# GpSimd's indirect transfers in a four-layer mixture-of-experts kernel: a wait for the preceding pair's landing in place of a wait for the tile two slots back

## The chip, the cores and the metric

The kernel runs on one core of one Trainium2 chip. The metric is the device time of one execution in microseconds (us), as the median of three runs. The engines are named as in the profile: PE is TensorE (PEld its weight loads), DVE VectorE, ACT ScalarE, POOL GpSimd, SP SyncE. Here SP issues all plain DMAs, and POOL issues all indirect ones.

## The reference

Six sublayers are applied to x, which is 8 x 256 rows of 128 columns (2048 rows):

```python
x = x + 0.5 * _L0_ffn_ref(_layernorm(x), ...)
x = x + _L0_attn_ref(_layernorm(x), ...)
x = x + 0.5 * _L0_ffn_ref(_layernorm(x), ...)
x = x + 0.5 * _L1_ffn_ref(_layernorm(x), ...)
x = x + _L1_attn_ref(_layernorm(x), ...)
x = x + 0.5 * _L1_ffn_ref(_layernorm(x), ...)
```

Each of the four feed-forward sublayers is a mixture of 8 experts in which every row goes to its two best:

```python
xn = rms_norm(x, norm_scale)
scores = xn @ w_router.T
scores_topk, idx = jax.lax.top_k(scores, 2)
up = moe_linear(xf, ids, w_up)             # xf: each row twice, row i gets W[ids[i]]
u, gate = jnp.split(up, 2, axis=-1)
down = moe_linear(u * jax.nn.silu(gate), ids, w_down)
out = jnp.sum(down * weights, axis=-2)
return out + skip
```

The hidden width is 256 in the first two and 352 in the last two. L0 attention is squared-ReLU attention within 256 rows, L1 attention is a causal linear attention with 16 heads.

## The kernel before

The 2048 rows are four groups of 512 (group index b or g). A feed-forward sublayer s (0 to 3) of one group is a **phase**: the group's 1024 (row, expert) pairs are sorted by expert into 15 tiles of 128 rows, a tile per **slot**. There are 16 phases in the order sublayer by sublayer and group by group within one, so 240 slots (SLOTS). While PE multiplies the tiles of one phase, all other work (routing, attention, combining) of the other groups is placed between the slots by tables of offsets, ROUTE, ATTENTION and COMBINE, counted in slots from the end of a group's last phase. Each engine has one instruction stream written in the order of the slots, and executes it in order; semaphores tie the streams together.

The path of one group from one phase to the next touches POOL several times:

- **Gather** (`gather`, L514, slots 3 to 6 after the phase's end): y_rows<-y_dram. The expert results, stored in DRAM by SP, are fetched back in row order, by eight indirect transfers of 128 rows of 512 bytes: four pairs, each pair of one block c of 128 rows (first and second expert). Semaphore gathered[b][c // 2]. In the last phase part of the tiles is gathered by `gather_early` (L531), which had no wait for a slot.
- **Combine** on DVE (L722), in two halves h0 and h1, each of which waits for two pairs of the gather. For sublayer 0 the halves are 8 and 10 slots after the phase's end.
- **Attention**, after sublayers 0 and 2. POOL computes a_rstd (L538) with a power function, and for L1 attention four products of 128x512 (L547, attention<-attention), from which ACT makes kv_hi and DVE kv_lo, which PE sums.
- **Route** for the next sublayer: POOL computes b_rstd (L486), then come the normalised rows rms_out (DVE L708), scores, top two, and the row positions pos (DVE L832, rows_of; semaphore pos_ready).
- **Scatter** (L495, route's offset "scatter"): rows_dram<-rms_out. The 512 normalised rows are written into sorted order in DRAM, by four pairs of indirect transfers. Semaphore scattered[g]. SP then waits for all eight and loads the rows back (L386, rows<-rows_dram), four tiles at a time, in the same queue that issues the loads of the expert weights (L400, up<-in_up, four slots ahead).

POOL's stream holds 16 scatters and 15 gathers of four pairs and the four pairs of gather_early, 128 pairs in all. Below, scatter k and gather k are those of phase k, counted from 0.

Before every pair stands `pace(t)`: the pair of slot t waits until ACT's SiLU (L581, semaphore silu_done) has finished the tile of slot t-2. It holds nothing else back: where POOL is late, the pairs follow one another at once.

## Time and profile before

| | us |
|---|---|
| median of 3 runs | 762.65 |
| the three runs | 762.65, 761.97, 771.69 |
| span of the profiled execution, first to last instruction | 751.7 |
| median less that span (start and end of an execution, outside the span) | 10.95 |
| PE busy in the span | 616.4 |
| POOL busy in the span | 318.2 |

The time of the profiled execution as a whole is not listed beside its span, so the difference to the median stands for what lies around it. POOL is busy while it generates the descriptors of a transfer; the time in which the DMA engines move the data and signal the semaphore is in no engine's busy time.

### The profile page before, as it was taken

How to read it: one execution, taken by the hardware profiler on the slowest of the kernel's cores; microseconds unless marked ns; L12 is line 12 of the kernel's file. 1: busy time of each engine (PE TensorE's matmuls, PEld its weight loads, DVE VectorE, ACT ScalarE, POOL GpSimd, SP SyncE). 2: the span in 40 equal slices, each digit the busy share in tenths (PEclk: the TensorE clock that was granted, in tenths of full speed). 3: DMA queues.
4: the chain of work that ended last, by engine and by line, in shares of the span. 5: the costliest groups of instructions: out<-in, count | busy, mean ns of one | idle time of the engine just before them, and what ended most of it. 6: DMA issues, size and time to landing. Idle time of an engine off the chain costs nothing.

```text
span 751.7 us, 15429 instructions
## 1 busy us (share of the span) xinstructions
PE 616.4 (82%) x4590; PEld 567.3 (75%) x4590; DVE 404.3 (54%) x1385; ACT 263.8 (35%) x549; POOL 318.2 (42%) x352
## 2 busy tenths in 40 slices
PE   2597888959969598767879779798898989888987
PEld 1386777848759488667779779697887979877987
DVE  6744343815528146342445335297796876954446
ACT  2233342523524333322333223443634435323331
POOL 4535444261441633544350534514615736344134
PEclk9999899989989989786988889899999999998999
DMA  7578576635626347564765657475564575556853
GB/s 253 149 221 260 170 204 212 194 110 148 187 75 199 116 143 222 155 208 135 216 197 149 190 156 214 136 207 164 173 201 132 159 232 156 181 166 224 261 157 76
DMA packets 113268, 133.57 MB, mean 178 GB/s; under 512 B 10931, under 2 KB 76227, under 8 KB 112806
## 3 DMA queue, kind: packets, MB, share of 16 engines
q1 hardware_dynamic: 104998, 115.79, 52.6%
q0 software_dynamic: 8192, 16.79, 7.4%
q8 instruction: 42, 0.69, 0.4%
q14 instruction: 36, 0.29, 0.1%
HBM read 103.83 MB, written 28.71 MB: 176 GB/s over the span
## 4 chain that ended last, share of the span: by engine, by line
PE 59%; DVE 12%; another core or an unknown queue 12%; issue 7%; ACT 7%; POOL 2%; DMA 0%; DVEq 0%; ACTq 0%
PE up_gate L1029 18%; PE up_gate L1022 11%; PE y L983 10%; PE side L1110 3%; PE y L985 3%; PE side L1044 2%; ACT hidden L581 2%; POOL b_rstd L486 2%; PE side L1060 2%; DVE hidden L686 2%; PE side L1126 2%; ACT x_res L598 2%; DVE rms_out L708 1%; DVE kv_lo L872 1%
## 5 line engine op out<-in xcount | busy, mean ns | idle before, releaser
L686 DVE TENSOR_TENSOR hidden<-up_gate,hidden 128x256 f32<-128x256 f32 (+1 forms) x240 | 115.7, 488 | 252.0 <-ACT hidden L581 125.0
L1029 PE MATMUL up_gate<-rows_T,up 128*128 128x128 f32 x1440 | 194.5, 286 | 26.0 <-issue 14.0
L1029 PEld LDWEIGHTS up_gate<-rows_T,up 128*128 128x128 f32 x1440 | 181.4, 200 | 32.4 <-issue 19.6
L495 POOL DMA_INDIRECT rows_dram<-rms_out,rows_of x128 | 130.1, 1016 | 171.8 <-DVE rows_of L832 90.5
L581 ACT ACTIVATE hidden<-up_gate 128x256 f32<-128x256 f32 (+1 forms) x240 | 104.3, 436 | 279.8 <-PE up_gate L1022 103.0
L514 POOL DMA_INDIRECT y_rows<-y_dram,rows_of x120 | 121.9, 1016 | 85.3 <-ACT hidden L581 46.1
L1022 PE MATMUL up_gate<-rows_T,up 128*128 128x128 f32 x960 | 139.7, 291 | 16.5 <-ACT rows_T L586 9.6
L1022 PEld LDWEIGHTS up_gate<-rows_T,up 128*128 128x128 f32 x960 | 126.7, 203 | 24.7 <-issue 22.1
L983 PE MATMUL y<-down,hidden 128*128 x480 | 78.7, 288 | 8.2 <-DVE hidden L686 6.0
L486 POOL TENSOR_TENSOR b_rstd<-b_var,minus_half 128x8 f32<-128x8 f32 x16 | 26.8, 1674 | 121.6 <-DVE b_var L703 121.5
L983 PE MATMUL y<-down_a,hidden 128*128 x480 | 76.3, 283 | 0.0
L983 PEld LDWEIGHTS y<-down,hidden 128*128 128x128 f32 x480 | 67.3, 202 | 11.1 <-issue 11.1
L586 ACT ACTIVATE rows_T<-side,norm 128x512 f32<-128x512 f32 x64 | 42.2, 660 | 75.8 <-remote 39.8
L983 PEld LDWEIGHTS y<-down_a,hidden 128*128 128x128 f32 x480 | 66.4, 200 | 0.0
L574 ACT ACTIVATE y_tile<-y 128x512 f32<-128x512 f32 x64 | 36.4, 569 | 35.8 <-PE y L985 22.0
L985 PE MATMUL y<-down_b,hidden 96*128 x240 | 47.9, 281 | 0.0
L1044 PE MATMUL side<-ident,rows 128*128 128x128 f32 x236 | 38.3, 284 | 2.5 <-DVE scores L770 1.5
L985 PEld LDWEIGHTS y<-down_b,hidden 96*128 96x128 f32 x240 | 37.9, 198 | 0.0
L1110 PE MATMUL side<-attention 128*128 128x256 f32 x64 | 20.8, 492 | 19.4 <-DVE attention L888 18.4
L1055 PE MATMUL side<-ident,rms_out 128*128 128x128 f32 x64 | 12.4, 326 | 29.6 <-DVE rms_out L708 15.3
L1110 PEld LDWEIGHTS side<-attention 128*128 128x128 f32 x64 | 15.9, 256 | 23.4 <-DVE attention L888 18.9
L1055 PEld LDWEIGHTS side<-ident,rms_out 128*128 128x128 f32 x64 | 8.4, 165 | 31.4 <-issue 23.3
(188 smaller groups left out, 700.4 us busy)
## 6 DMA issues: line engine op xcount, KB each, us to landing
up<-in_up SPq DMA_DIRECT2D x120, 352.0 KB
up<-in_up SPq DMA_DIRECT2D x120, 256.0 KB
rows<-rows_dram SPq DMA_DIRECT2D x47, 256.0 KB, 3.0
y_dram<-y_tile SPq DMA_DIRECT2D x45, 256.0 KB, 2.5
rows_dram<-zeros SPq DMA_DIRECT2D x12, 256.0 KB, 3.6
rows<-rows_dram SPq DMA_DIRECT2D x16, 192.0 KB
y_dram<-y_tile SPq DMA_DIRECT2D x15, 192.0 KB
rows_dram<-rms_out,rows_of POOLq DMA_INDIRECT x128
```

The lines of the kernel that those rows point to most:

```text
L486: pool.tensor_tensor(b_rs[:, :], b_ve[:, :], mhalf[:, :], ALU.pow).then_inc(b_rstd, 1)
L495: pool.indirect_dma_start(out=xg_d[g], out_offset=bass.IndirectOffsetOnAxis(ap=pos[g][:, at:at + 1], axis=0), in_=xs(Z, GROUPS[g][c // TB] ...
L514: pool.indirect_dma_start(out=gath[b % 2][:, (TB * k2 + c) * P:(TB * k2 + c + 1) * P], out_offset=None, in_=y_d[g], in_offset=bass.Indirec ...
L581: act.activation(hid[n % 4][:, 0:w], src, ACT.Silu).then_inc(silu_done, 1)
L586: act.activation(xgT[r % 3][:, 0:n * P], S[2][:, 0:n * P], ACT.Copy, scale=wn[:, LAYER[s]:LAYER[s] + 1]).then_inc(s2_free, 1)
L686: dve.tensor_tensor(h, u, h, ALU.mult).then_inc(mult_done, 1)
L983: last = pe.matmul(y, hid[n % 4][:, c * P:(c + 1) * P], w, start=(c == 0), stop=(l == 0 and c == 1))
L985: last = pe.matmul(y, hid[n % 4][0:96, 2 * P:3 * P], dn1b[:, bass.ds(v * P, P)], start=False, stop=True)
L1022: last = pe.matmul(U[q % 3][:, i * P:(i + 1) * P], upW[n % RING][:, at:at + P], rows_, start=True, stop=True)
L1029: last = pe.matmul(U[q % 3][:, c * P:(c + 1) * P], upW[n % RING][:, at + c * P:at + (c + 1) * P], rows_, start=True, stop=True)
L1044: last = pe.transpose(S[2][:, c * P:(c + 1) * P], xg[r % 4][:, c * P:(c + 1) * P], ident[:, :])
L1110: last = pe.matmul(S[1 - q][:, c * SEQ:(c + 1) * SEQ], R[4 + q][:, t * HID + c * P:t * HID + (c + 1) * P], R[6 + q][:, t * SEQ:(t + 1) * S ...
```

## The change

`pace` and its wait on silu_done go. In its place every pair remembers its semaphore and the count that the semaphore has when both its transfers have landed (`pair_landed`), and before the next pair POOL waits for that (`wait_for_pair`). gather_early, which had no pacing, gets the same wait. The other waits (pos_ready, y_stored, combined) stay.

```diff
-            def pace(t):
-
-                if 1 < t <= SLOTS:
-                    pool.wait_ge(silu_done, t - 1)
+            landing = []
+
+            def pair_landed(sem, count):
+
+                landing[:] = [(sem, count)]
+
+            def wait_for_pair():
+
+                for sem, count in landing:
+                    pool.wait_ge(sem, count)
...
-                    pace(t)
+                    wait_for_pair()
                     for at in (2 * c, 2 * c + 1):
                         pool.indirect_dma_start(out=xg_d[g], out_offset=bass.IndirectOffsetOnAxis(ap=pos[g][:, at:at + 1], axis=0),
                                                 in_=xs(Z, GROUPS[g][c // TB], c % TB * P, P), in_offset=None,
                                                 bounds_check=TILES[g] * P - 1, oob_is_err=False).then_inc(scattered[g], 16)
+                    pair_landed(scattered[g], 32 * (CH[g] * (turns(s1, g) - 1) + c + 1))
...
-                    pace(t)
+                    wait_for_pair()
                     i = TB * GROUPS[g].index(b) + c
                     for k2 in range(2):
...
+                    pair_landed(gathered[b][c // 2], 16 * TB * s + 32 * (c % 2 + 1))
...
+                wait_for_pair()
                 for k2 in range(2):
                     at = 2 * c + k2
...
+                pair_landed(gathered[b][c // 2], 16 * TB * s + 32 * (c % 2 + 1))
```

No instruction changes its place on any engine; only what POOL's pairs wait for differs. Two places of POOL's stream show it. The first is the round of POOL in the L0 attention part, from the last pair of scatter 5 (rows_dram1) over gather 3 (y_rows1<-y_dram3) to the first pair of scatter 6. Before:

```order
L495 DMA rows_dram1<-rms_out,rows_of1 1920x128 [waits silu_done]
L495 DMA rows_dram1<-rms_out,rows_of1 1920x128
L514 DMA y_rows1<-y_dram3,rows_of3 128x128 [waits y_stored3,combined,y_stored2,silu_done,y_stored1,y_stored0]
L514 DMA y_rows1<-y_dram3,rows_of3 128x128
L514 DMA y_rows1<-y_dram3,rows_of3 128x128 [waits silu_done]
...
L486 TENSOR_TENSOR b_rstd<-b_var,minus_half 128x8 [waits b_var]
L538 TENSOR_TENSOR a_rstd<-a_var,minus_half 128x4 [waits ln1_var]
L495 DMA rows_dram2<-rms_out,rows_of2 1920x128 [waits silu_done,pos_ready]
```

And after:

```order
L501 DMA rows_dram1<-rms_out,rows_of1 1920x128 [waits scattered1]
L501 DMA rows_dram1<-rms_out,rows_of1 1920x128
L521 DMA y_rows1<-y_dram3,rows_of3 128x128 [waits y_stored3,combined,y_stored2,scattered1,y_stored1,y_stored0]
L521 DMA y_rows1<-y_dram3,rows_of3 128x128
L521 DMA y_rows1<-y_dram3,rows_of3 128x128 [waits gathered3_0]
...
L492 TENSOR_TENSOR b_rstd<-b_var,minus_half 128x8 [waits b_var]
L548 TENSOR_TENSOR a_rstd<-a_var,minus_half 128x4 [waits ln1_var]
L501 DMA rows_dram2<-rms_out,rows_of2 1920x128 [waits gathered3_1,pos_ready]
```

Each silu_done has become a wait for the landing of the pair before, also across the border from scatter to gather; b_rstd and a_rstd stand behind all eight pairs as before.

The second place is in the L1 attention part, the end of gather 10 (y_rows0<-y_dram2), scatter 12 (rows_dram0) and the first two products of L1 attention. Before:

```order
L514 DMA y_rows0<-y_dram2,rows_of2 128x128 [waits silu_done]
L514 DMA y_rows0<-y_dram2,rows_of2 128x128
L495 DMA rows_dram0<-rms_out,rows_of0 1920x128 [waits silu_done,pos_ready]
L495 DMA rows_dram0<-rms_out,rows_of0 1920x128
L547 TENSOR_TENSOR attention<-attention 128x512 [waits v_ready,phi_ready]
```

And after:

```order
L521 DMA y_rows0<-y_dram2,rows_of2 128x128 [waits gathered2_1]
L521 DMA y_rows0<-y_dram2,rows_of2 128x128
L501 DMA rows_dram0<-rms_out,rows_of0 1920x128 [waits gathered2_1,pos_ready]
L501 DMA rows_dram0<-rms_out,rows_of0 1920x128
L557 TENSOR_TENSOR attention<-attention 128x512 [waits v_ready,phi_ready]
```

The products are queued behind the gather and the scatter's first pair in both; the pairs ahead of them now wait for landings.

## Rows read from the trace of the kernel before

**Rows 1.** The page: span, busy time, chain by engine, hardware DMA queue.

```profile
span 751.7 us, 15429 instructions
PE 616.4 (82%) x4590; PEld 567.3 (75%) x4590; DVE 404.3 (54%) x1385; ACT 263.8 (35%) x549; POOL 318.2 (42%) x352
PE 59%; DVE 12%; another core or an unknown queue 12%; issue 7%; ACT 7%; POOL 2%; DMA 0%; DVEq 0%; ACTq 0%
q1 hardware_dynamic: 104998, 115.79, 52.6%
```

**Rows 2.** The chain that ended last: start us, us, what.

```profile
200.81 3.20 another core or an unknown queue
...
207.48 6.49 another core or an unknown queue
```

**Rows 3.** Timeline of POOL, one round: start us, us, engine line op.

```profile
196.90 1.06 POOL L495 DMA_INDIRECT rows_dram<-rms_out,rows_of  x1 [6.86 <-DVE rows_of L832]
198.27 0.99 POOL L495 DMA_INDIRECT rows_dram<-rms_out,rows_of  x1 [0.30 <-issue]
...
207.23 1.04 POOL L514 DMA_INDIRECT y_rows<-y_dram,rows_of  x1 [0.30 <-issue]
...
219.37 1.00 POOL L514 DMA_INDIRECT y_rows<-y_dram,rows_of  x1 [0.31 <-issue]
229.14 1.67 POOL L486 TENSOR_TENSOR b_rstd<-b_var,minus_half 128x8 f32<-128x8 f32 x1 [8.78 <-DVE b_var L703]
...
245.09 1.06 POOL L495 DMA_INDIRECT rows_dram<-rms_out,rows_of  x1 [6.86 <-DVE rows_of L832]
```

**Rows 4.** Timeline of DVE: the positions for which scatter 6 waited.

```profile
244.11 0.17 DVE L832 CAST rows_of<-rows_of_f 128x8 int32<-128x8 f32 x1
```

**Rows 5.** Timelines: last transfer of a set, and who waited for its landing.

```profile
548.17 0.99 POOL L495 DMA_INDIRECT rows_dram<-rms_out,rows_of  x1 [0.30 <-issue]
550.44 0.38 SPq L386 DMA_DIRECT2D rows<-rows_dram  x1
...
689.55 0.98 POOL L495 DMA_INDIRECT rows_dram<-rms_out,rows_of  x1 [0.31 <-issue]
694.60 0.38 SPq L386 DMA_DIRECT2D rows<-rows_dram  x1
...
742.83 0.99 POOL L531 DMA_INDIRECT y_rows<-y_early,early_rows_of  x1 [0.30 <-issue]
745.72 0.61 DVE L722 SCALAR_TENSOR_TENSOR x_res<-y_rows,w_first,x_res 128x128 f32<-128x128 f32 x2 [2.16 <-DMA y_rows<-y_early,early_rows_of]
```

**Rows 6.** Timelines: first scatter, combine h1 of gather 0, scatter 3.

```profile
19.62 1.21 POOL L495 DMA_INDIRECT rows_dram<-rms_out,rows_of  x1 [7.96 <-issue]
...
95.41 0.59 DVE L722 SCALAR_TENSOR_TENSOR x_res<-y_rows,w_first,x_res 128x128 f32<-128x128 f32 x2
...
100.11 1.06 POOL L495 DMA_INDIRECT rows_dram<-rms_out,rows_of  x1 [0.27 <-issue]
```

**Rows 7.** Timeline of POOL: first pairs of scatters 7 and 11.

```profile
292.15 1.07 POOL L495 DMA_INDIRECT rows_dram<-rms_out,rows_of  x1 [13.33 <-ACT hidden L581]
...
459.98 1.02 POOL L495 DMA_INDIRECT rows_dram<-rms_out,rows_of  x1 [19.28 <-DVE rows_of L832]
```

**Rows 8.** Timeline of POOL, L1 attention part, scatters 12 and 15.

```profile
486.48 2.10 POOL L547 TENSOR_TENSOR attention<-attention 128x512 f32<-128x512 f32 x2
...
519.48 1.09 POOL L514 DMA_INDIRECT y_rows<-y_dram,rows_of  x1 [0.44 <-issue]
...
534.16 1.02 POOL L495 DMA_INDIRECT rows_dram<-rms_out,rows_of  x1 [1.74 <-ACT hidden L581]
...
545.35 1.08 POOL L547 TENSOR_TENSOR attention<-attention 128x512 f32<-128x512 f32 x1
...
567.85 1.08 POOL L514 DMA_INDIRECT y_rows<-y_dram,rows_of  x1 [0.45 <-issue]
...
678.28 1.02 POOL L495 DMA_INDIRECT rows_dram<-rms_out,rows_of  x1 [0.31 <-issue]
```

**Rows 9.** Timelines: first pair of gather_early; the last addition.

```profile
732.15 1.00 POOL L531 DMA_INDIRECT y_rows<-y_early,early_rows_of  x1 [11.43 <-issue]
...
748.28 0.69 DVE L733 TENSOR_TENSOR x_res<-x_res,side 128x512 f32<-128x512 f32 x1 [1.30 <-PE side L1173]
```

## The prediction

> **What bounds the kernel now.** I read the page first. PE is busy 82% of the span and stands for 59% of the chain that ended last; POOL is busy 42% and stands for 2% [rows 1]. Read so, POOL's transfers are far from the bound. But 12% of the chain is "another core or an unknown queue" [rows 1], some 90 us that no engine's work explains, so I looked where in the chain it lies. It comes in pieces such as the 3.20 us at 200.81 and the 6.49 us at 207.48 [rows 2]. In both, ACT had finished and PE's tile had been issued, and the tile's signal came late. The timeline of POOL shows what goes on beside: both lie in a dense run of indirect transfers, one every 1.3 us, that begins at 196.90 and goes over from scatter 5 to gather 3 [rows 3]. The other long pieces that I looked up lie in such runs too. So the kernel before pays up to 90 us for something that goes with many indirect transfers in flight, and the change, which never has more than two in flight, may give that back. This speaks for the change and is in the sum below, in full.
>
> Against it stands a time that no busy row shows: how long a pair takes until its landing is known to POOL. It decides the sum.
>
> **The price of a pair.** Generating two transfers takes from 196.90 to 198.27 + 0.99 = 199.26 [rows 3]: 2.35 us. The landing, from the end of the second generation to whoever waited for it: 550.44 - 549.16 = 1.28 us, 694.60 - 690.53 = 4.07 us, and for a gather 745.72 - 743.82 = 1.90 us [rows 5]. The low end is a quiet moment of the queues, the high end one with loads beside. The hardware queue is at work for 52.6% of the span [rows 1], so neither end is typical; I take the gather row, 1.9 us. Restart: pos was written at 244.11 + 0.17 = 244.28 and scatter 6, which waited for it, began at 245.09 [rows 3, 4]: 0.8 us, which a dense run hides in its gap of 0.3. Together P = 2.35 + 1.9 + 0.8 = 5.05, taken as 5.0 us from pair to pair, where a dense run needs 2 x 1.3 = 2.6. Bounds for P as a mean: 2.35 + 1.28 + 0.8 = 4.4 below, and with half of the pairs at each of the two scatter rows 2.35 + 2.7 + 0.8 = 5.8 above.
>
> This is where a page bears on it. "DMA: Bandwidth & Descriptors" of the Trainium skill, section "Anatomy of one DMA — SWDGE (gpsimd) path", gives such a transfer a fixed 2.0 us, most of it the write's receipt, plus bytes over 436e3. For the 64 KB here that is 2.15 us from issue, an estimate from that page, against 550.44 - 548.17 = 2.27 in the quiet row and 5.05 in the loaded one [rows 5]: the trace agrees with it only in the quiet case. By the page P would be 1.3 + 2.15 + 0.8 = 4.25 (estimate), and the total would come out near 741 us.
>
> **What hangs on POOL's queue.** 128 pairs at 5.0 us are 640 us, where POOL was busy 318 us, generation of all of them included [rows 1]. So POOL turns from an engine with 58% idle into one in which nearly every round is a chain. I follow the queue in six parts. PE stalls are assumed gone everywhere.
>
> (a) *Start to scatter 3.* Scatters 0 to 2 and gather 0 follow each other without a gap: the positions for scatters 1 and 2 are ready by the time POOL gets there, and the waits on silu_done that had held scatter 2 are gone. From 19.62 there are 15 steps of P, the last pair's generation and landing (2.35 + 1.9), then combine h1, after which scatter 3 came 100.11 - 95.41 = 4.70 later, over a_rstd [rows 6]. 19.6 + 75 + 4.25 + 4.7 = 103.6 against 100.1: **+3.5**.
>
> (b) *Scatter 3 to scatter 7, four rounds, 192.0 us* (100.11 to 292.15) [rows 6, 7]. In each, b_rstd stands behind all eight pairs, and the next positions depend on it: from b_rstd to the next scatter 245.09 - 229.14 = 15.95 us [rows 3], in which PE runs at its pace without a stall, so it stays. Before, POOL had ended its pairs at 220.37 and b_rstd waited 8.8 us for its data [rows 3]; that slack is eaten. A round is 7 x 5.0 + 2.35 + 15.95 = 53.3 us; four are 213.2: **+21.2**. The stalls lie inside the eight pairs, so that their end buys nothing here.
>
> (c) *Scatter 7 to scatter 11, four rounds, 167.8 us* (292.15 to 459.98) [rows 7]. No attention; b_rstd stands between scatter and gather, and the chain from it to the next positions, without its stalls, runs beside the gather and is no longer than that. A round is then 8 pairs, 40.0 us: 160 in all, **-7.8**. This is what of the stalls is earned.
>
> (d) *Scatter 11 to scatter 12, 74.2 us* (459.98 to 534.16). The products of L1 attention wait behind scatter 11 and gather 9: they come 37.35 us after the scatter's start, where it was 486.48 - 459.98 = 26.5. From there to gather 10 PE's pace rules, 519.48 - 486.48 = 33.0, and the gather's four pairs take 20 us where scatter 12 came 14.7 after it [rows 7, 8]: 37.35 + 33.0 + 20 = 90.35, **+16.2**.
>
> (e) *Scatter 12 to scatter 15, three rounds, 144.1 us* (534.16 to 678.28). The last product comes behind the third pair, 2 x 5.0 + 2.35 = 12.35 after the start, against 545.35 - 534.16 = 11.19; the product itself and two of its fellows lie in the landing waits. From it to the next gather 567.85 - 545.35 = 22.5, unchanged, then 20 us of gather [rows 8]. Three times 54.85 is 164.6: **+20.4**.
>
> (f) *End.* The rows of the last phase are loaded 3 x 5.0 + 2.35 + 1.9 = 19.25 us after scatter 15 starts, against 694.60 - 678.28 = 16.3 [rows 5, 8]; SP already waited for them, with the weight loads queued behind: **+2.9**. gather_early takes 19.25 against 745.72 - 732.15 = 13.6; of these 5.7 us about 1.2 are hidden, since the last addition waited 1.30 for PE [rows 5, 9]: **+4.5**.
>
> Sum: 3.5 + 21.2 - 7.8 + 16.2 + 20.4 + 2.9 + 4.5 = +60.9. Span 751.7 + 60.9 = 812.6, and with the 10.95 us around it **823.6 us, 824**. What is removed, a wait that POOL's sequencer makes, costs nothing itself.
>
> Of the chain that I sum, 15 + 28 + 32 + 11 + 18 + 6 = 110 steps are P. Each 0.1 us of P is 11 us, and with P at 5.0 - 61/110 = 4.45 the change does nothing.
>
> **Rivals.**
>
> 1. *The landings are quick.* With the pairs spread out and PE often idle, the weight loads leave the queues quiet, and P is near its lower bound 4.4: +60.9 - 66 = -5, 757 us, no change. For it: the quiet row recurs wherever SP had stopped issuing. Against: the same weights must still be moved, and the scatters start while PE runs and asks for them. The page's 4.25, and its total of 741, would be this rival's extreme.
>
> 2. *The stalls are what counts, and POOL isn't the chain.* The other side: the 12% go, 90 us [rows 1], and landings stay hidden under the schedule's slack. 762.65 - 90 = 673; it needs eight pairs and the work behind them within a round that is 48.2 us now (196.90 to 245.09) and would be some 38 without the two pieces of rows 2: 7P + 18.3 below 38 asks for P below 2.9, less than the generation and the quiet landing. A gain of over 2% asks for 15.3/110 below the even point, P under 4.3, which is under the lower bound, unless my chains are wrong: if in (b) b_rstd could go ahead of the gather's last pairs, for instance, which its place in the queue forbids. It is the case in which I have misread what depends on what.
>
> 3. *The stalls stay.* If PE's late signals come with every indirect transfer and not with the number in flight, (b) is unchanged, but (c) doesn't shrink: its stalls of some 10 us a round come beside waits already there. With half of that on the path +20, 844 us.
>
> 4. *The change does nothing* because the pairs' landing is as a rule past when the next is due. 745.72 and 550.44 speak against it: a dense run issues every 1.3 us, far ahead of any landing.
>
> **How the numbers follow.** My forecast (P from 4.6 to 5.4, 780 to 868): 0.60. Rival 3: 0.12. Rival 1 and 4 together: 0.15. Rival 2, in full or in part: 0.13. Within 2% (747.4 to 777.9), about what a measurement of this kernel can tell from no change, lie rivals 1 and 4: 0.15; faster is rival 2: 0.13; slower the rest, 0.72. The range reaches down to rival 1 and up over rival 3 to P of 5.4: 755 to 868.
>
> **What the profile after would show.** POOL's transfers in pairs, 4.4 to 5.8 us from pair to pair, each with an idle time before it put down to DMA or to issue of 2 to 3 us, in place of 0.3. The share "another core or an unknown queue" under 4%, with more of the chain on POOL and DMA. In (b), b_rstd right behind the last gather transfer, with DVE idle before L708 and L722, and rounds of 53 us. In (d), L547 some 37 us after scatter 11's start. I am wrong if the mean step is under 4.45, if b_rstd still waits for b_var in (b), or if unexplained pieces of the chain stay.

## The result, and the profile after

| | before | after |
|---|---|---|
| median, us | 762.31 (759.75 to 771.69, 4 runs) | 878.22 (871.85 to 883.42, 4 runs) |
| ratio | | 1.149, 95% interval 1.141 to 1.158 |
| profiled execution, its time, us | not on record | 871.85 |
| its span, us | 751.7 | 870.1 |

The change makes the kernel 15% slower, by 116 us; 61 had been forecast. In the experiments below a median is of all runs, while a ratio and its interval leave out runs more than 1.5% above the quickest of their kernel. The page of the changed kernel, to be held against [rows 1]: span, busy time, hardware queue, chain by engine, and three groups (busy and mean ns, then idle time before them and what ended most of it).

```profile
span 870.1 us, 15430 instructions
PE 622.5 (72%) x4590; PEld 578.2 (66%) x4590; DVE 405.3 (47%) x1385; ACT 268.5 (31%) x549; POOL 317.7 (37%) x352
q1 hardware_dynamic: 104998, 115.79, 45.0%
DMA 44%; POOL 18%; issue 18%; PE 14%; DVE 4%; POOLq 1%; ACT 1%; DVEq 0%; ACTq 0%
L501 POOL DMA_INDIRECT rows_dram<-rms_out,rows_of x128 | 130.1, 1017 | 239.9 <-DMA rows_dram<-rms_out,rows_of 134.0
L521 POOL DMA_INDIRECT y_rows<-y_dram,rows_of x120 | 121.9, 1016 | 197.4 <-DMA y_rows<-y_dram,rows_of 135.4
L718 DVE TENSOR_SCALAR rms_out<-x_res,b_meanvar,b_rstd 128x128 f32<-128x128 f32 x64 | 17.9, 347 | 132.9 <-POOL b_rstd L492 132.9
```

POOL is busy for the same 318 us, and yet the chain has changed hands: PE went from 59% to 14%, and DMA (that is, POOL waiting for landings) from 0 to 44%. "Another core or an unknown queue", 12% before, isn't in the list any more. These are waits in ACT and DVE that the view of waits puts down to "remote"; the piece of 6.49 us in [rows 2] is one. In the kernel before it looked so:

```profile
203.35 1.05 PE L1022 MATMUL up_gate<-rows_T,up 128*128 128x128 f32 x8
213.99 0.38 ACT L581 ACTIVATE hidden<-up_gate 128x256 f32<-128x256 f32 x1 [6.51 <-remote]
```

This SiLU (L581) waits for one semaphore only, the one that PE raises behind the eight products; PE's records of them end at 204.40, and ACT went on at 213.99. Below these waits are called unexplained.

In the changed kernel the idle time ended by landings, 134.0 + 135.4, is 269 us. Busy shares show none of this; the idle columns do.

One round of (b) on POOL, the counterpart of [rows 3]:

```profile
202.37 1.00 POOL L521 DMA_INDIRECT y_rows<-y_dram,rows_of  x1 [2.86 <-DMA y_rows<-y_dram,rows_of]
...
207.89 1.00 POOL L521 DMA_INDIRECT y_rows<-y_dram,rows_of  x1 [3.22 <-DMA y_rows<-y_dram,rows_of]
...
212.53 1.00 POOL L521 DMA_INDIRECT y_rows<-y_dram,rows_of  x1 [2.34 <-DMA y_rows<-y_dram,rows_of]
213.83 1.00 POOL L521 DMA_INDIRECT y_rows<-y_dram,rows_of  x1 [0.30 <-issue]
214.86 1.68 POOL L492 TENSOR_TENSOR b_rstd<-b_var,minus_half 128x8 f32<-128x8 f32 x1
...
232.49 1.06 POOL L501 DMA_INDIRECT rows_dram<-rms_out,rows_of  x1 [8.53 <-DVE rows_of L842]
```

Pairs start 5.52 and 4.64 us apart. b_rstd has lost its wait of 8.78 [rows 3] and stands right behind the gather's last transfer. The same round on DVE:

```profile
198.83 0.16 DVE L713 SCALAR_TENSOR_TENSOR b_var<-b_var,b_meanvar 128x4 f32<-128x4 f32 x1
...
216.57 1.12 DVE L718 TENSOR_SCALAR rms_out<-x_res,b_meanvar,b_rstd 128x128 f32<-128x128 f32 x4 [16.47 <-POOL b_rstd L492]
```

b_var was there at 198.99, and DVE stood idle for 16.47 us until POOL came round to b_rstd.

The steps' length varies with what the DMA engines carry. The third and the fourth pair of scatter 0, then rows of a round of (c), from scatter 8 to scatter 9:

```profile
30.11 0.97 POOL L501 DMA_INDIRECT rows_dram<-rms_out,rows_of  x1 [2.03 <-DMA rows_dram<-rms_out,rows_of]
...
34.39 0.97 POOL L501 DMA_INDIRECT rows_dram<-rms_out,rows_of  x1 [2.03 <-DMA rows_dram<-rms_out,rows_of]
...
386.55 1.08 POOL L501 DMA_INDIRECT rows_dram<-rms_out,rows_of  x1 [2.90 <-DMA y_rows<-y_dram,rows_of]
...
393.56 0.97 POOL L501 DMA_INDIRECT rows_dram<-rms_out,rows_of  x1 [3.95 <-DMA rows_dram<-rms_out,rows_of]
...
399.20 0.97 POOL L501 DMA_INDIRECT rows_dram<-rms_out,rows_of  x1 [3.39 <-DMA rows_dram<-rms_out,rows_of]
...
429.40 1.02 POOL L501 DMA_INDIRECT rows_dram<-rms_out,rows_of  x1 [3.99 <-DMA y_rows<-y_dram,rows_of]
```

30.11 to 34.39 is a quiet step, 4.28 us; 386.55 to 393.56 is 7.01, 393.56 to 399.20 is 5.64, and the round's eight pairs take 42.85 in all, 5.36 each. The same stretches in the view by windows (us, then busy us and instructions of PE, PEld, DVE, ACT and POOL, granted clock, busy share of the DMA engines, GB/s):

```profile
30.11:34.39 4.28, 2.34 (x22) 2.06 (x21) 0.83 (x4) 1.38 (x4) 1.94 (x3) 1.00 0.09 31
386.55:393.56 7.01, 5.13 (x44) 4.76 (x43) 3.51 (x17) 2.68 (x6) 2.09 (x3) 1.00 0.63 208
```

The DMA engines are busy for 0.09 of the quiet step and for 0.63 of the long one. It is so throughout: of the 99 steps from a scatter pair to a scatter pair or a gather pair to a gather pair, the 11 below 4.5 us have a mean share of 0.19, the 28 of 6 us and more one of 0.75. By the formula that "DMA: Bandwidth & Descriptors" of the Trainium skill, section "Anatomy of one DMA — SWDGE (gpsimd) path", gives for one transfer, a step is 4.25 us (estimate): the trace agrees with this in the quiet row, 4.28, and in none of the loaded rows shown.

The borders of the six parts of the forecast, the first pairs of scatters 3, 7 and 11, the first product behind scatter 11, and scatters 12 and 15:

```profile
115.72 1.11 POOL L501 DMA_INDIRECT rows_dram<-rms_out,rows_of  x1 [0.21 <-issue]
341.84 1.06 POOL L501 DMA_INDIRECT rows_dram<-rms_out,rows_of  x1 [14.57 <-DVE rows_of L842]
523.24 1.02 POOL L501 DMA_INDIRECT rows_dram<-rms_out,rows_of  x1 [4.20 <-DVE rows_of L842]
565.00 1.08 POOL L557 TENSOR_TENSOR attention<-attention 128x512 f32<-128x512 f32 x1
618.68 1.02 POOL L501 DMA_INDIRECT rows_dram<-rms_out,rows_of  x1 [4.06 <-DMA y_rows<-y_dram,rows_of]
788.93 1.07 POOL L501 DMA_INDIRECT rows_dram<-rms_out,rows_of  x1 [6.03 <-DMA y_rows<-y_dram,rows_of]
```

| part | before | after | change | forecast |
|---|---|---|---|---|
| (a) to scatter 3 | 100.1 | 115.7 | +15.6 | +3.5 |
| (b) 3 to 7 | 192.0 | 226.1 | +34.1 | +21.2 |
| (c) 7 to 11 | 167.8 | 181.4 | +13.6 | -7.8 |
| (d) 11 to 12 | 74.2 | 95.4 | +21.3 | +16.2 |
| (e) 12 to 15 | 144.1 | 170.3 | +26.1 | +20.4 |
| (f) to the end | 73.4 | 81.2 | +7.7 | +7.4 |
| span | 751.7 | 870.1 | +118.4 | +60.9 |

### The profile page after: what moved, and what is told of

Its sections match the earlier page's. It is cut to its first block, busy times and chain, and to the rows that moved or that the text cites. A ratio compares the mean times of both kernels' runs of the same rounds, so it can differ in the third digit from the quotient of the medians.

```text
span 870.1 us, 15430 instructions
## 1 busy us (share of the span) xinstructions
PE 622.5 (72%) x4590; PEld 578.2 (66%) x4590; DVE 405.3 (47%) x1385; ACT 268.5 (31%) x549; POOL 317.7 (37%) x352
## 4 chain that ended last, share of the span: by engine, by line
DMA 44%; POOL 18%; issue 18%; PE 14%; DVE 4%; POOLq 1%; ACT 1%; DVEq 0%; ACTq 0%
DMA y_rows<-y_dram,rows_of 20%; DMA rows_dram<-rms_out,rows_of 20%; POOL rows_dram L501 7%; POOL y_rows L521 7%; PE up_gate L1039 5%; PE y L993 3%; POOL b_rstd L492 2%; PE up_gate L1032 2%; DMA y_rows<-y_early,early_rows_of 1%; DMA y_dram<-y_tile 1%; POOL attention L557 1%; PE y L995 1%; PE side L1054 1%; DMA rows<-rows_dram 1%; DVE rms_out L718 1%
## 5 line engine op out<-in xcount | busy, mean ns | idle before, releaser
L501 POOL DMA_INDIRECT rows_dram<-rms_out,rows_of x128 | 130.1, 1017 | 239.9 <-DMA rows_dram<-rms_out,rows_of 134.0
L1039 PE MATMUL up_gate<-rows_T,up 128*128 128x128 f32 x1440 | 197.7, 290 | 11.5 <-DVE hidden L696 7.5
L1039 PEld LDWEIGHTS up_gate<-rows_T,up 128*128 128x128 f32 x1440 | 185.4, 204 | 17.8 <-DVE hidden L696 8.8
L521 POOL DMA_INDIRECT y_rows<-y_dram,rows_of x120 | 121.9, 1016 | 197.4 <-DMA y_rows<-y_dram,rows_of 135.4
L1032 PE MATMUL up_gate<-rows_T,up 128*128 128x128 f32 x960 | 143.1, 297 | 5.0 <-issue 3.6
L1032 PEld LDWEIGHTS up_gate<-rows_T,up 128*128 128x128 f32 x960 | 130.9, 209 | 13.1 <-issue 10.8
L993 PEld LDWEIGHTS y<-down,hidden 128*128 128x128 f32 x480 | 69.6, 209 | 72.0 <-issue 72.0
L718 DVE TENSOR_SCALAR rms_out<-x_res,b_meanvar,b_rstd 128x128 f32<-128x128 f32 x64 | 17.9, 347 | 132.9 <-POOL b_rstd L492 132.9
L1065 PE MATMUL side<-ident,rms_out 128*128 128x128 f32 x64 | 15.3, 384 | 65.3 <-DVE rms_out L718 63.2
L1065 PEld LDWEIGHTS side<-ident,rms_out 128*128 128x128 f32 x64 | 10.6, 196 | 67.4 <-DVE rms_out L718 56.7
L603 ACT ACTIVATE z_T<-side,norm 128x512 f32<-128x512 f32 x16 | 11.0, 686 | 135.7 <-PE side L1065 129.4
L492 POOL TENSOR_TENSOR b_rstd<-b_var,minus_half 128x8 f32<-128x8 f32 x16 | 26.9, 1681 | 71.0 <-DVE b_var L713 70.9
L1054 PEld LDWEIGHTS side<-ident,rows 128*128 128x128 f32 x236 | 28.6, 146 | 36.2 <-DMA rows<-rows_dram 21.2
## 6 DMA issues: line engine op xcount, KB each, us to landing
rows<-rows_dram SPq DMA_DIRECT2D x16, 192.0 KB
y_dram<-y_tile SPq DMA_DIRECT2D x15, 192.0 KB
```

Source lines behind the costliest of these rows:

```text
L492: pool.tensor_tensor(b_rs[:, :], b_ve[:, :], mhalf[:, :], ALU.pow).then_inc(b_rstd, 1)
L501: pool.indirect_dma_start(out=xg_d[g], out_offset=bass.IndirectOffsetOnAxis(ap=pos[g][:, at:at + 1], axis=0), in_=xs(Z, GROUPS[g][c // TB] ...
L521: pool.indirect_dma_start(out=gath[b % 2][:, (TB * k2 + c) * P:(TB * k2 + c + 1) * P], out_offset=None, in_=y_d[g], in_offset=bass.Indirec ...
L993: last = pe.matmul(y, hid[n % 4][:, c * P:(c + 1) * P], w, start=(c == 0), stop=(l == 0 and c == 1))
L1032: last = pe.matmul(U[q % 3][:, i * P:(i + 1) * P], upW[n % RING][:, at:at + P], rows_, start=True, stop=True)
L1039: last = pe.matmul(U[q % 3][:, c * P:(c + 1) * P], upW[n % RING][:, at + c * P:at + (c + 1) * P], rows_, start=True, stop=True)
```

## The experiments

Each set of kernels ran beside the kernel before on the same chip. In four of the five sets that took 756 to 762 us, in the second 644.5. This difference became the most telling measurement, and is taken up below. The sets in which the kernel before took 756 to 762 us are called the usual condition, the second set the quick one. The ratios are always to the kernel before of the same set.

**Set 1** (before: 757.2 us).

*nowait*: neither the old wait nor the new one.

```diff
-                if 1 < t <= SLOTS:
-                    pool.wait_ge(silu_done, t - 1)
+                return
```

> The kernel before without pace, and with no wait for a landing: the change's one half alone. Theory A (the 15% are the landing waits, in POOL's in-order queue): taking pace away costs little, 755 to 790 us, with the unexplained pieces of the chain (PE's late signals) as long as before or longer, since runs of transfers get denser. Theory B (the loss comes from pace having kept the transfers away from other work, and the landing wait only adds to it): 800 us or more.

782.2 us, ratio 1.031 (1.024 to 1.037), in theory A's range. Dropping the pacing alone costs 25 us, and the unexplained share of the chain rises to 16%: a queue that runs freely is worse than one that is paced. The changed kernel has no unexplained share, so these 3% aren't shown to be a part of its 15%.

*lag2*: a pair waits for the pair before the preceding one, four transfers in flight (the counts split over two semaphores).

```diff
-                landing[:] = [(sem, count)]
+                landing.append((sem, count))
...
-                for sem, count in landing:
-                    pool.wait_ge(sem, count)
+                if len(landing) > 1:
+                    pool.wait_ge(*landing[-2])
```

> The changed kernel, but each pair waits for the pair before the preceding one, so up to four transfers are in flight (the semaphores of scatters and gathers are split by pair parity). Theory A: a landing of 2 to 5 us lies beside the next pair's generation, the step from pair to pair falls from some 5.5 us to 2.6 to 3.5, and the total to 690 to 745 us if four in flight are too few for PE's late signals, 750 to 775 if they are enough for them. Theory B (pace's removal costs): 820 us or more.

754.8 us is the median of ten runs between 737 and 763, no clear difference from the kernel before (757.2); the ratio of 0.981 (0.974 to 0.988) rests on the two quickest of the ten. Pairs are 3.2 us apart in scatters and 2.8 in gathers in the mean, the chain of landings is gone, but 9% of the chain is still unexplained. One pair more in flight is worth over 120 us against the change.

*scatter_only*: the landing waits in the scatters only; the gathers have pace(t) again, gather_early none. The scatter's first pair no longer waits for the gather before it, nor the gather's for the scatter, so a wait at the border is in neither half.

> Landing waits between the pairs of a scatter only; the gathers keep pace, gather_early has no wait. Theory A: some six in ten of the added time, since the scatters are half of the pairs and their landings stand before gathers and products too, 805 to 835 us; PE's late signals come back only in the gathers. Rival: if the gathers' landings alone hold b_rstd and the combines, under 785 us.

769.8 us, 1.018 (1.013 to 1.023), the rival's number. That scatters cost little doesn't follow yet: 8% of the chain is unexplained here too, so the two effects are mixed.

*after_small*: the changed kernel with the loads of the up weights cut to 32 columns after the first six tiles of each layer (it leaves out most of these weights).

```diff
+                u = w if n < RING or LAYER1 <= n < LAYER1 + RING else PAD
-                sp.dma_start(upW[n % RING][:, 0:w], (up0, up1)[l][:, bass.ds(v * w, w)])
+                sp.dma_start(upW[n % RING][:, 0:u], (up0, up1)[l][:, bass.ds(v * w, u)])
```

> The changed kernel with the weight loads cut: after the first six tiles of either layer only 32 of 512 or 704 columns are loaded (the expert results are those of stale weights). Theory A' (the pair step was priced too low because the landing competes with the weight loads): every pair step falls to the quiet 4.3 us of scatters and 4.6 of gathers, and the total by some 110 x 1 us to 750 to 790 us. Rival (the landing is slow by itself, by its receipt from DRAM or POOL's restart): steps stay at 5.4 to 5.6 us on average and the total above 850 us.

816.7 us in one run, between the two. The hardware queue's share falls from 45.0% to 21.7%, and the 32 steps of (c) from 181.4 to 161.5 us, from 5.67 to 5.05 a step, where a quiet one is 4.28. The weight loads make about half of what a step takes beyond the quiet row; what the rest is was not told apart (the loads and stores of rows and results are still there). Neither A', which had the quiet step and 750 to 790 us, nor its rival came true.

**Set 2** (before: 644.5 us, 642.7 to 652.0, 11 runs).

*gather_only*: the counterpart of scatter_only.

```diff
                         if turns(s1, g) == 1:
                             pool.wait_ge(zero_stored[g], 16 * ((TILES[g] + 3) // 4))
-                    wait_for_pair()
+                    pace(t)
```

> The counterpart of scatter_only: only the pairs of the gathers and of gather_early wait for the pair before them, the scatters are paced as before. Theory S (slack): in each round one half of the cost is taken up by time that POOL had to spare (8.8 us before b_rstd in (b)), and only what goes beyond it counts. Gather steps of about 5.4 us: 3 us a round in (b), nothing in (c), 7 us before scatter 12 and in each of the three rounds of (e), 5 at the end: about +45, 785 to 820 us, so that this kernel and scatter_only together come to much less than the change. Rival S' (sum): a pair costs the same wherever it stands, and since scatter_only came out 13 us above the kernel before and the change 115, this kernel takes the rest, 845 to 870 us.

745.4 us, 1.156 (1.148 to 1.163). The numbers were written for a kernel before of 757; as a difference, +101 us, it is what rival S' had (88 to 113), and not what slack had (28 to 63). Set 4 takes this up again.

*one_flight*: every single transfer waits for the one before (shown for the scatters; the gathers got the like).

```diff
                     for at in (2 * c, 2 * c + 1):
+                        if at % 2:
+                            pool.wait_ge(scattered[g], 32 * (CH[g] * (turns(s1, g) - 1) + c) + 16)
```

> The changed kernel with every single transfer waiting for the one before, so twice as many landings. Theory A (the cost is the number of landing steps on POOL's chain, at some 2.8 us each beyond a generation with its gap): some 110 to 118 steps more, each about 2.8 us, 1150 to 1220 us. Rival B (the landings take long because of what is in flight beside them, and get as quick as the quiet ones, 1.3 to 1.9 us, when everything thins out): 1.5 us or less a step more, 1000 to 1080 us.

1138.4 us in one run, 12 us short of theory A's range and far from B's: 262 us over the changed kernel's 876 (measured in set 4) for 110 more landings on the chain, 2.4 us each. The pair steps of a set grew from 5.5 and 5.4 us to 7.5 and 7.8. Its granted clock is lower too, 0.784 where the changed kernel has 0.866, so not all of the 2.4 need be landing.

*hoist*: b_rstd before the third pair of the gather.

```diff
-                if o == route_at(s1, b)["root"]:
+                if o == route_at(s1, b)["root"] - (3 if s1 == 1 else 0):
```

> The changed kernel with b_rstd of the four rounds of (b) put between the second and the third pair of the gather, in place of behind the fourth. Its data is ready by then (b_var stands at 198.99 us in the round in which b_rstd starts at 214.86). Theory H, as in the prediction: b_rstd is what heads the way to the next positions, so it and all that follows come 10 to 11 us earlier in each of four rounds: 825 to 840 us. Rival H' (the combine): the same DVE stream has both halves of the combine, which wait for the gather's last pair, between rms_out and the positions, so only the 2 to 3 us between the last landing and the end of the combine are saved: 860 to 870 us.

856.7 us, 1.326 (1.318 to 1.334), 3 us under H' and far from H. One round of it on DVE:

```profile
207.18 1.11 DVE L718 TENSOR_SCALAR rms_out<-x_res,b_meanvar,b_rstd 128x128 f32<-128x128 f32 x4 [9.59 <-POOL b_rstd L492]
...
218.23 0.61 DVE L732 SCALAR_TENSOR_TENSOR x_res<-y_rows,w_first,x_res 128x128 f32<-128x128 f32 x2 [7.98 <-DMA y_rows<-y_dram,rows_of]
```

Counted from the round's first scatter (175.45 here, 177.52 in the changed kernel), rms_out comes 7.3 us earlier than at 216.57, and the second half of the combine, behind it in DVE's stream, waits 7.98 us for the gather's last landing. This round is as long as before, 55.0 us in both. b_rstd was held up, but it was not alone in that.

*lag2_pace*: lag2 with pace(t) kept beside it.

> lag2 (a pair waits for the pair before the preceding one) with the old wait for the tile two slots back kept beside it. Theory C (what lag2 gained, it gained by fewer transfers in flight, and what it lost, nothing): the pacing spreads the runs further and the late signals of PE get rarer still: 735 to 750 us, faster than lag2. Rival D (the pacing adds waits to a queue that is late already): 752 to 765 us, no better than lag2's 754.84.

661.4 us, 1.025 (1.019 to 1.031). Both theories had been written for a kernel before of 757, and neither number came; beside 644.5 even this limit costs. The chain of gather_only here, and under it that of the kernel before as it ran in set 3 (before_again):

```profile
PE 29%; DMA 22%; POOL 17%; issue 16%; DVE 10%; ACT 4%; POOLq 1%; SPq 0%; DVEq 0%; ACTq 0%
```

```profile
PE 59%; DVE 14%; another core or an unknown queue 9%; issue 9%; ACT 7%; POOL 2%; DMA 0%; DVEq 0%; ACTq 0%
```

None of the four kernels traced in set 2 has a wait for "remote", and none of their chains an unexplained share (that of lag2_pace covers only the last 8% of its span).

**Set 3** (before: 762.3 us) repeated the main kernels; the quick condition didn't come back.

> The kernel before once more, for a trace of it on the chip on which it took 644.5 us, where all runs until then had shown 752 to 772. Theory X (the late signals of PE inside the dense runs of transfers, 12% of the chain in the first trace, are the whole difference, and that chip doesn't show them): a span of about 643 us and a share of another core or an unknown queue under 1%. Rival Y (the chips differ in the clock alone): the share stays near 12%, and PE's busy time differs in the ratio of the clocks. On a chip of the first kind both expect 750 to 765 us and 12%.

759.6 us, with an unexplained share of 9% where 12% had been expected: a condition of the usual kind, on which both theories say the same.

> The changed kernel beside the kernel before on this chip. Theory X: the changed kernel hangs on POOL's chain of landings, which the late signals hardly touch, so that its time is the same on either kind of chip, 860 to 880 us; where the kernel before takes 644.5 the ratio is then 1.33 to 1.37, where it takes 757 it is 1.14 to 1.16. Rival Y: both kernels get faster by the same ratio of 0.85, and the changed one takes about 740 us on the quicker chip.

879.8 us, 1.147 (1.139 to 1.156).

> lag2 beside the kernel before on this chip. Theory X: what lag2 gained (0.981) it gained on the late signals, so where they are absent only its cost is left, as in lag2_pace: 1.01 to 1.04 of the kernel before. Rival: lag2 is better in itself, 0.98 there too.

759.3 us, the median of ten runs between 740 and 765; 0.979 (0.970 to 0.988) is again the ratio of its two quickest.

> scatter_only beside the kernel before on this chip. Theory X: it came out at 1.018 only because it paid 4.4 of its own and won back a part of the late signals; where there are none its price shows in full: 1.05 to 1.12, and with the 1.156 of gather_only the two make up most of the change (1.33 and more). Rival S (slack, each half alone fits into idle time of POOL): 1.01 to 1.03.

781.3 us, 1.019 (1.011 to 1.027). Rival S had this; X's 1.05 to 1.12 was for the quick condition. In the usual condition the results of set 1 stand.

**Set 4** (before: 755.7 us) repeated those of set 2, to see them in the usual condition.

> gather_only beside the kernel before on this chip. Where the kernel before shows late signals of PE (757 to 762 us so far on three chips): theory X (the halves keep a part of the chain of landings and lose a part of the late signals) expects 785 to 815 us, 1.03 to 1.07, and with the 1.019 of scatter_only less than half of the change's 1.149, so that the cost comes mostly from both standing in one chain. Rival S' (sum): 845 to 870 us. Where the kernel before takes 644: 1.156 again.

755.1 us, 0.996 (0.992 to 1.001), lower than either theory had it: the same edit that costs 16% in set 2 costs nothing here.

> hoist beside the kernel before on this chip: b_rstd two gather pairs earlier in (b). Theory H' (the combine is what the next positions wait for, behind the gather's last landing): 2 to 4 us a round, 860 to 870 us against the 878 and 880 of the changed kernel, 1.13 to 1.14. Theory H (b_rstd alone): 825 to 840 us.

854.8 us, 1.132 (1.126 to 1.137), 5 us under H'; in set 2 it was 856.7.

> lag2 with the old pacing kept beside it, on this chip. Where the kernel before shows late signals: theory C (fewer in flight and the pairs spread) 730 to 750 us, 0.96 to 0.98; rival D (the pacing adds nothing but waits) 755 to 775. Where the kernel before takes 644: 1.025 again.

732.6 us, 0.972 (0.965 to 0.978), as theory C had it, and the best of all kernels in this condition.

> The changed kernel once more. On a chip with late signals 870 to 885 us. On one where the kernel before takes 644, theory X expects the chain of landings to be as long as ever, 860 to 880 us, 1.33 to 1.37; rival Y (everything is faster there) about 740.

876.3 us, 1.160 (1.151 to 1.168). hoist is 21.5 us quicker beside it. Its (b) takes 216 us, where the changed kernel's takes 235 here and 226 in the first trace, so 2 to 5 us a round in the mean; H' had 2 to 4. The rounds differ: in set 2, against the first trace, they gained 2.5, 0.0, 0.6 and 9.3 us. Why the last one gains what H had for all was not looked into.

**Set 5** (before: 757.8 us).

*slide*: as many in flight as in the change, two at most, but each single transfer waits for the last but one (counts over two semaphores).

```diff
-                    wait_for_pair()
                     for at in (2 * c, 2 * c + 1):
+                        wait_for_last_but_one()
...
```

> The changed kernel with its wait made sliding: each single transfer waits for the landing of the last but one, so that as many are in flight as in the changed kernel, two at most, but one is being generated while the other lands. Theory X (the cost is the length of a step, the gain the small number in flight): a pair takes 2 x (1.0 + about 1.9 + 0.8 restart) / 2 = 3.7 to 4.2 us in place of 5.4, so 110 steps save 130 to 190 us of the changed kernel's 876, and the late signals stay away as there: 700 to 745 us, below the kernel before where that takes 757. Where the kernel before takes 644: 690 to 720, slower than it. Rival Z (a wait for one landing costs what a wait for two does, since the landings are slow because of what else is in the queues): steps of 5 and more, 840 to 870 us.

768.7 us, 1.011 (1.005 to 1.017): 24 us over its range, 108 under the changed kernel of set 4. A piece of POOL's timeline and the chain:

```profile
357.43 1.02 POOL L522 DMA_INDIRECT y_rows<-y_dram,rows_of  x1 [0.31 <-issue]
359.43 1.01 POOL L522 DMA_INDIRECT y_rows<-y_dram,rows_of  x1 [0.99 <-DMA y_rows<-y_dram,rows_of]
360.75 1.01 POOL L522 DMA_INDIRECT y_rows<-y_dram,rows_of  x1 [0.30 <-issue]
362.73 1.01 POOL L522 DMA_INDIRECT y_rows<-y_dram,rows_of  x1 [0.97 <-issue]
```

```profile
DMA 40%; PE 21%; issue 17%; POOL 10%; DVE 10%; ACT 2%; POOLq 1%; DVEq 0%; ACTq 0%; SPq 0%
```

Here two transfers take 359.43 to 362.73 = 3.3 us; over the 32 steps of (c), 148.9 us, it is 4.65 a pair, where 3.7 to 4.2 had been expected. Rival Z, with 5 and more and 840 to 870 us, is refuted. No unexplained share, as in the changed kernel.

*slide_hoist*: both edits.

> slide with b_rstd two gather pairs earlier, as in hoist. Theory H': worth at most 2 to 4 us a round of (b) where POOL's chain still binds, 5 to 15 us below slide. Rival (with shorter steps b_rstd waits for its data there as in the kernel before, and holds up the last two gather pairs): equal to slide or up to 15 us slower.

752.3 us, 0.991 (0.987 to 0.996), 16 us under slide, just past the 5 to 15 of H', and just below the kernel before. It comes in (b), 204.9 us in slide and 183.8 here: 5.3 a round, over the 2 to 4 of H'.

**What the sets say together.** The view of waits of the kernel before, the unexplained ones in ACT and DVE (us in total, times, longest), and of lag2:

```profile
ACT hidden L581 <- remote: 60.6, 15, 7.2
ACT rows_T L586 <- remote: 39.8, 11, 6.0
DVE hidden L686 <- remote: 26.1, 7, 6.6
```

```profile
ACT hidden L592 <- remote: 46.4, 11, 7.7
ACT rows_T L597 <- remote: 32.0, 9, 6.0
DVE hidden L697 <- remote: 24.7, 5, 8.6
```

And of gather_only in set 4:

```profile
ACT hidden L595 <- remote: 40.5, 11, 6.7
ACT rows_T L600 <- remote: 26.9, 6, 7.4
```

Where they lie in time tells more. With the landing waits in the scatters only, all 23 unexplained waits of scatter_only stand beside a run of gathers; with them in the gathers only, all 18 of gather_only in set 4 stand beside a run of scatters. In the kernel before they stand beside both. One from scatter_only, and the gather transfer at its start:

```profile
267.57 1.00 POOL L526 DMA_INDIRECT y_rows<-y_dram,rows_of  x1 [0.31 <-issue]
277.95 0.94 ACT L593 ACTIVATE hidden<-up_gate 128x256 f32<-128x256 f32 x3 [10.82 <-remote]
```

| kernel | in flight | usual condition, us (unexplained waits) | set 2, us (unexplained waits) |
|---|---|---|---|
| nowait | any | 782 (yes) | |
| before | any, paced | 756 to 762 (yes) | 644.5 (no trace) |
| lag2 | 4 | 755 (yes) | |
| lag2_pace | 4, paced | 733 (yes) | 661 (none) |
| scatter_only | 2 in scatters | 770 (yes) | |
| gather_only | 2 in gathers | 755 (yes) | 745 (none) |
| slide | 2 | 769 (none) | |
| hoist | 2 | 855 (none) | 857 (none) |
| after | 2 | 876 to 880 (none) | |
| after_small | 2 | 817 (none) | |
| one_flight | 1 | | 1138 (none) |

In the usual condition five kernels with at most two transfers in flight (after, after_small, hoist, slide, slide_hoist) leave no such wait in seven traces, and every kernel with more in flight anywhere shows them. one_flight shows none either, but it ran in set 2, where no kernel does, whatever it has in flight. And only kernels with more than two in flight somewhere differ between the conditions: lag2_pace by 71 us, the kernel before by 113, gather_only by 10, hoist by 2.

My reading is that the change does two things of opposite sign. It takes away a loss that the kernel before has in the usual condition, 757 - 644.5 = 113 us. And it puts a chain of landings in its place, which costs, against a kernel without the loss, some 876 - 644.5 = 232 us. The net is the 116 to 121 measured. Two parts of this are argued and not shown. That the changed kernel takes 876 in the quick condition too rests on hoist, which took the same in both; it wasn't run there. And that the 113 are the unexplained waits isn't shown, since the kernel before has no trace in set 2. lag2_pace has one in both: its span is 67.9 us shorter in the quick condition, the granted clock 0.979 in place of 0.941, and 26.9 of the 67.9 are PE's own busy time (585.7 and 612.6 us for the same products). So a part of such a loss is time at a lower clock, and whether the waits bring the clock down or something else brings both was not tested. A low clock alone doesn't bring the waits: gather_only has 0.932 in set 2 and none of them.

The gather's half bears the reading out: it costs 101 us in set 2 and nothing in the usual condition, where it may pay for itself with the part of the loss that it ends. The rest would then be 131 us, for the scatters' half and the waits at the borders between the two; of that only the 13 to 19 of scatter_only in the usual condition were measured, and how much appears only when all form one chain isn't told apart.

That the unexplained waits come with more than two transfers in flight is shown for the usual condition; by what way a transfer holds them up, and what makes the condition, is open. Two of the sets carry the same chip number, one at 644.5 and one at 755.7, so the number alone doesn't tell them apart, and nothing in the traces names a cause.

## Why the prediction was wrong

The direction held, and so did the mechanism (POOL becomes a chain of landings, the unexplained pieces go); 878 lies above the range's end of 868.

**The step that failed is the price of a pair**, P = 5.0 us. In the sum it stands for 110 steps. Measured, these 110 take 600.4 us, 5.46 each: 50 of the 57.5 us by which the span was missed. In (c), where b_rstd and the positions hold up next to nothing, it is 181.4 / 32 = 5.67. I had taken the landing of the one gather row of [rows 5], 1.90 us, as the middle. The quiet scatter row was right (idle 2.03 = 1.28 + 0.8, to within 0.05), and typical rows are far from it: 2.9, 3.4, 3.95, where 1.9 + 0.8 = 2.7 had been assumed. With P at 5.45 the sum is 60.9 + 50 = 111 and the span 862.6; with the 6.3 of (b) below it is 868.9, where 870.1 was measured. The bound above, 5.8, held; the range of my forecast ended at P = 5.4, inside that bound, and so cut off the case that came.

Part by part: **(a)** +12 over the forecast, nearly all of it steps: scatter 3 came 12.1 us later than forecast, and the 15 steps took 86.3 us in place of 75. **(b)** +12.9 over it. The order of things was as told, b_rstd right behind the gather, DVE idle before rms_out. Half of the miss is steps; the other half is a second step of the prediction that failed, the way from b_rstd to the next scatter, which I had said "stays" at 15.95: in the round shown it is 232.49 - 214.86 = 17.63, and from 16.3 to 18.8 in the four, +6.3 in all. This stretch in the view by windows, before and after:

```profile
229.14:245.09 15.95, 15.40 (x129) 14.13 (x128) 13.69 (x62) 8.16 (x18) 2.68 (x2) 1.00 0.68 200
214.86:232.49 17.63, 13.03 (x92) 12.07 (x93) 13.32 (x60) 5.70 (x12) 2.68 (x3) 0.76 0.30 82
```

In the 10 us ahead of b_rstd PE was busy for 8.8 to 10 in all four rounds before; in the changed kernel it is busy for none of them in any round, and the granted clock falls to between 0.64 and 0.50 there. In the stretch behind b_rstd the clock, 1.00 in all four rounds before, is 0.74 to 0.79. Of the four, the longest (18.82 us) has the lowest clock, 0.74, and the shortest (16.25) the highest, 0.79. So the clock goes with the 6.3; that it makes them was not tested by a run. That b_rstd is the head was half of the truth: with it moved, the combine waits in its place (hoist), and a round gains 2 to 5 us in the mean, not 9. **(c)** is where the price of P turned the sign: forecast 40.0 a round against 41.95 before, measured 45.4. The gain I had booked there, -7.8, was the stalls' end; they did end, and the price of P took more than they gave. **(d)** The product came 565.00 - 523.24 = 41.8 after scatter 11, forecast 37.35; the 4.4 are the miss but for 0.7. **(e)** +5.7 over 18 steps, 0.3 a step. **(f)** right to 0.3, in part by luck: the three steps of its scatter took 13.7 us in place of 15, the three of gather_early 15.9.

**A second term was wrong and partly hid it**: 10.95 us for what lies around a span. It was the difference of a median and the span of another execution. Where both belong to one, it is 871.85 - 870.1 = 1.75. With 1.75 around it, the execution traced before would have taken some 753 us, 9 below the median. The sum added to the median, 762.65 + 60.9 = 823.5, gives the same forecast, by luck; but against the traced execution of 871.85 the 9 us hid a part of the miss.

**The rivals.** 1, quick landings: no, the steps are 4.3 only where the DMA engines have little else to do; even with most of the weights left out they were 5.05 in (c). 2, the stalls go and POOL isn't the chain: the stalls do go (what that gives back would be 113 us by the reading above, where it had 90), but POOL is the chain. 3, the stalls stay: refuted, none in any kernel with two in flight. 4, no effect because landings are past anyway: refuted, 269 us of POOL's idle time end with one. My sign of failure for P looked to one side only, "under 4.45"; the miss was on the other.

## What to carry to other kernels

Waiting for the landing of what was just issued costs the whole landing each time: with the same two in flight, waiting for the last but one was 108 us quicker here than waiting for the last pair, and ended 1% above the kernel before in place of 15% (slide, in the usual condition). Take a landing's price from rows in the stretches where the waits will stand, several of them, not from one: here an idle time of 2.0 us in quiet steps and 3 to 4 in loaded ones, 110 times over, was 50 of the 57.5 us missed. And where a chain has a share that no engine explains, look first at which of the experiments lose it: it may be a loss of the size of the change, with a sign of its own.

## What the runs showed of the hardware

- In the usual condition, with more than two indirect transfers of 128 rows in flight on POOL's queue, ACT and DVE stood in unexplained waits of up to 7.2 us in the kernel before (15 + 11 + 7 waits in the rows above, 126.5 us of idle time), up to 8.6 in lag2 and 10.8 in scatter_only, and they stood beside the transfers that were not limited. With at most two in flight there was none in five kernels. In the quick condition none of the four kernels traced had any.
- The same program took 644.5 us in one set and 755 to 762 in the others, granted clock 0.98 and 0.92 to 0.93, while hoist, with two transfers in flight, took the same in both to 0.3% (856.7 and 854.8).
- Two in flight, one generated while the other lands, gives a transfer per 2.3 us in (c) (148.9 / 64); waiting for both gives one per 2.8 (181.4 / 64).
- A pair step (two generations, landing, restart) was 4.28 us with the DMA engines busy for 0.09 of it and 7.01 with 0.63; in the mean 5.05 in (c) with most weight loads left out (hardware queue 21.7%), 5.67 with all (45.0%).
- The stretch from b_rstd to the next scatter took 15.95 us at a granted clock of 1.00, and 16.3 to 18.8 at 0.74 to 0.79, after PE had done nothing for the 10 us ahead of it (granted clock there 0.50 to 0.64, full speed being 1.00).
